# Three one-pass products in place of one float32 product for layer 3's maps, and grouped float32r products in layer 4

## The chip, the cores and the metric

The kernel runs on one core of a Trainium2 chip. The metric is the time of one execution on the device in microseconds (us), as the median of several runs. TensorE (PE) multiplies matrices, VectorE (DVE) and ScalarE (ACT) work element by element, GpSimd (POOL) does a little of that, and SyncE (SP) issues nearly all DMAs from one queue, in the order in which they are written. Each engine runs its own instructions in order; semaphores tie the engines together.

## The reference

A graph with 3125 nodes of 256 features and 50000 edges goes through a layer norm, a relu and four SAGE layers; the input is added at the end.

```python
def _sage_conv(x, src, dst, Wl, Wr, b):
    agg = segment_sum(x[src], dst, num_segments=n)
    deg = segment_sum(ones_like(dst), dst, num_segments=n)
    mean = agg / maximum(deg, 1.0)[:, None]
    return mean @ Wl + x @ Wr + b
h = maximum(_layernorm(x), 0.0)
h = relu(_sage_conv(h, src, dst, Wl1, Wr1, b1))     # 256 -> 256
h = relu(_sage_conv(h, src, dst, Wl2, Wr2, b2))     # 256 -> 128
h = relu(_sage_conv(h, src, dst, Wl3, Wr3, b3))     # 128 -> 256
out = x + _sage_conv(h, src, dst, Wl4, Wr4, b4)     # 256 -> 256
```

## The kernel before

**Tiles and chunks.** The nodes are cut into 25 tiles of 128 (the last has 53) and into seven chunks: six of 512 nodes and one of 53. `ORDER` is 5, 6, 4, 3, 2, 1, 0; the text speaks of places, so place 1 is the short chunk (53 nodes) and places 0 and 2 to 6 are full. A dense table of edge counts, `counts`, stays on chip. Layer 1 is computed while this table is built; layers 2, 3 and 4 come after it, and this study is about layers 3 and 4.

**One place of a layer.** PE sums over all 25 source tiles (`add_sources`, called k = 0 to 24 by the loop `place` of the tensor block): for each tile the stored node values, as an f16 high part and an f16 low part, are multiplied by the counts, so a place of layer 3 is 49 products of 128x512 (the last tile takes one), and one of layer 4 is 98. The sums of a place lie in `agg_ps` or `window_ps`, in turn. DVE scales them by the reciprocal degrees into `aggT` (`scale_agg`, L1570). Then come the layer's two dense maps of the sums (`aggT`) and of the chunk's own values (`selfT`), called `lin`. PE issues `lin` of place q between the tiles of place q+1; the tables `rest` and `first_rests` say behind which tile k. In layer 3 that is k = 6 for place 2 and later, and place 2 carries two, `lin(3, 0)` at k = 2 and `lin(3, 1)` at k = 15, since place 1 is too short to hold any. The `lin` and the turns of the last place stand in the first place of the next layer, ahead of the tiles that `REST_AT` names.

**Layer 3 before.** `lin(3, q)` is four float32 products for a full chunk: two halves h of the 256 outputs, each W3 times `aggT` and W3 times `selfT`, in `lin_ps` (L2297). ACT makes the relu from `lin_ps` to `newT` (L1923) and an f16 high part (`high_part`, L1940); DVE makes the f16 low part (`low_part`, L1591). SP stores `newT` to memory (`hT_d`) and turns the four parts from feature-major to node-major by DMA transposes (`move_turned`, L913); places 1 and 6 are turned by PE instead (`turn`) and copied by DVE (`copy_turned`, L1608). On SP the order for place q is: wait for `lin`, load `selfT` of place q+1 (L852), load the reciprocal degrees of place q+1 (L864), store `newT`, issue the four transposes. So a load of `selfT` stands behind the transposes of the place before. DVE's order in layer 3 is `scale_agg(q)`, then for each half `low_part` and `copy_turned`; ACT's is the two relus, then the two high parts.

**Layer 4 before.** Its maps are already made with one-pass products. An operand a and a weight w are split into f16 parts and a sum part; eight f16 products of 256 columns give one half of the bank `last_ps(i)` and four float32r products of 256 columns (L2268) the other, tile by tile; DVE joins the two with fixed factors (`add_out`, L1692 and L1697). `split_operand` (L1733, L1737) and ACT's `operand_parts` (L2039) make the parts.

Of the kernel before, what the change touches and what calls it, by code (L numbers as in the profile page):

```python
# [26 lines left out]
def sage_stack_kernel(nc, x, src, dst, Wl1, Wr1, b1, Wl2, Wr2, b2, Wl3, Wr3, b3, Wl4, Wr4, b4, out):  # L27
# [240 lines left out]
    with ctx:  # L268
# [75 lines left out]
        partsT = sb("partsT", [P, 2, CH], f16)  # L344
        newH = sb("newH", [P, TPC, 2, D], f16)
        rdeg = sb("rdeg", [P, CH], f32)
        ident16 = sb("ident16", [P, P], f16)
        columns = sb("columns", [P, 18], f32)
# [4 lines left out]
        unscale_high, unscale_sum, unscale_up = (columns[:, i:i + 1] for i in (15, 16, 17))  # L353

# [252 lines left out]
        W4_parts = sem("W4_parts")  # L607
        W4_rests = sem("W4_rests")
# [13 lines left out]
        LIN = [0, 2, 1, 2, TPC]  # L622
# [56 lines left out]

        def in_second(l, q, h):  # L680

            return l == 3 and h == 1 and by_dma(q)
# [34 lines left out]
        REST_AT = {1: (2, 6, 11), 2: (2, 10), 3: (2, 6, 9)}  # L717
# [450 lines left out]
        def _(dve):  # L1168
# [417 lines left out]
            def low_part(l, q, h):  # L1586
                n, t = size_of(chunk_at(q))
                dve.wait_ge(high_done[l], TURNS[l] * q + h + 1)
                parts = parts_of(l, q, h)
                low = parts[:, 1, 0:n] if n == CH else parts[:, 0, TWIN:TWIN + n]  # L1590
                v.scalar_tensor_tensor(out=low, in0=(lin_ps if l == 1 else newT)[:, h, 0:n],  # L1591
                                       scalar=1 / SPLIT if l == 3 else scale[:, l - 1:l], in1=parts[:, 0, 0:n], op0=ALU.mult,
                                       op1=ALU.subtract).then_inc(low_done[l], 1)
# [107 lines left out]
            def scale_columns():  # L1701

                order.after(v.tensor_single_scalar(scale_up, scale[:, 2:3], SPLIT, ALU.mult))
                v.tensor_scalar(bias3_up, bT[:, 3:5], scale_up, None, ALU.mult)
                v.tensor_single_scalar(unscale_high, unscale[:, 3:4], (1 - 1 / SPLIT) / W4_UP, ALU.mult)
                v.tensor_single_scalar(unscale_sum, unscale[:, 3:4], 1 / SPLIT / W4_UP, ALU.mult)
                order.after(v.tensor_single_scalar(unscale_up, unscale[:, 3:4], 1 / SPLIT, ALU.mult))

            def split_weights():

                dve.wait_ge(W4_parts, 2)
# [5 lines left out]
                dve.wait_ge(lin_done[3], 2 * NCH)  # L1717
# [5 lines left out]
                for of in range(2):  # L1723
                    v.tensor_tensor(W4_rest[:, of, :, :], W4_sums[of][:, :, :].bitcast(f32), W4_high[of], ALU.subtract
                                    ).then_inc(W4_rests, 1)

            def split_operand(of, q):
# [3 lines left out]
                for k in range(2):  # L1731
                    dve.wait_ge(operand_high, 4 * q + 2 * (1 - of) + k + 1)
# [64 lines left out]
        def _(act):  # L1797
# [104 lines left out]
            def relu(l, q):  # L1902
                n, t = size_of(chunk_at(q))
                bias = {1: 0, 2: 2, 3: 3}[l]
# [7 lines left out]
                for h in range(NEW[l]):  # L1912
# [9 lines left out]
                    if l == 3:  # L1922
                        a.activation(newT[:, h, 0:n], source, ACT.Relu, bias=bias3_up[:, h:h + 1], scale=scale_up  # L1923
                                     ).then_inc(relu_done[l], 1)
                        continue
                    a.activation(newT[:, h, 0:n], source, ACT.Relu, bias=bT[:, bias + h:bias + h + 1]  # L1926
                                 ).then_inc(relu_done[l], 1)

            def high_part(l, q, h):
# [7 lines left out]
                else:  # L1937
# [3 lines left out]
                             scale=1 / SPLIT if l == 3 else scale[:, l - 1:l]).then_inc(high_done[l], 1)  # L1941
# [79 lines left out]

            for l in (2, 3):
                def place(q, bank):
                    relu(l, q)
# [32 lines left out]
        def _(pe):  # L2057
# [193 lines left out]
            def last_maps(q):  # L2251
# [3 lines left out]
                if isinstance(q, int) and q == 0:  # L2255
                    pe.wait_ge(W4_parts, 6)
                pe.wait_ge(operand_low, 4 * (q + 1))
                if not isinstance(q, int) or q > 0:
                    pe.wait_ge(out_made, both(q, TPC, 1))
                for i in range(t):  # L2260
                    node, wide = slice(i * P, i * P + rows_), slice(i * P, (i + 1) * P)
# [3 lines left out]
                    for j, (h, w) in enumerate(products):  # L2265
                        m(last_ps(i)[0:rows_, 0:D], h, w, start=(j == 0), stop=(j == len(products) - 1))  # L2266
                    for j, (of, k) in enumerate(((1, 0), (1, 1), (0, 0), (0, 1))):
                        last = m(last_ps(i)[:, D:2 * D], last_sums[:, of, k, wide], W4_sums[of][:, k, :],  # L2268
                                 start=(j == 0), stop=(j == 3))
                    last.then_inc(lin_done[4], 1)  # L2270

            def lin(l, q):

                if l == 4:
                    last_maps(q)
                    return
                n, t = size_of(chunk_at(q))
# [4 lines left out]
                if l == 3 and isinstance(q, int) and q == 0:  # L2282
                    pe.wait_ge(late_loaded, LATE)
# [6 lines left out]
                for h in range(1 if l == 2 else 2):  # L2290
                    cols = slice(h * P, (h + 1) * P)
                    if l == 2:
                        ops = [(Wr2_sb[:, k, :], selfT[:, k, 0:n]) for k in range(2)]
                    else:
                        ops = [(W3[:, 0, cols], aggT[:, 0, 0:n]), (W3[:, 1, cols], selfT[:, 0, 0:n])]
                    for i, (w, r) in enumerate(ops):
                        last = m(lin_ps[:, h, 0:n], w, r, start=(i == 0), stop=(i == len(ops) - 1))  # L2297
                    last.then_inc(lin_done[l], 1)
# [198 lines left out]
            def rest(l, q):  # L2497
# [3 lines left out]
                        3: {6: [lambda: lin(3, q)], 16: [lambda: turn(3, q, 0)], 22: [lambda: turn(3, q, 1)]},  # L2501
                        4: {8: [lambda: lin(4, q)]}}[l]

            def first_rests(l):
# [3 lines left out]
                        3: {2: [lambda: lin(3, 0)], 8: [lambda: turn(3, 0, 0)], 12: [lambda: turn(3, 0, 1)],  # L2508
                            15: [lambda: lin(3, 1)]},
                        4: {2: [lambda: lin(4, 0)], 12: [lambda: lin(4, 1)]}}[l]  # L2510

            for l in (2, 3, 4):
                def place(q, bank):
# [3 lines left out]
                    if l == 3 and isinstance(q, int) and q == 3:  # L2517
                        between = {2: [lambda: turn(3, 1, 0)], 5: [lambda: turn(3, 1, 1)], **between}
# [83 lines left out]
```

## Time and profile before

| | |
|---|---|
| median of 3 runs | 645.88 us (645.56 to 646.54) |
| the profiled execution | 645.63 us, of which the span from the first to the last instruction is 643.8 us |
| PE busy | 615.5 us, 96% of the span |
| DVE busy, ACT busy | 318.9 us (50%), 194.1 us (30%) |
| granted clock of PE, mean | 0.986 |

The profile is one execution. In it layer 3 begins at 383.9 us of the span; place 1 begins at 397.10, place 2 at 398.34. Matmuls are pipelined: the duration of one contains some 0.16 us that the next one overlaps, so the pace of PE is read from the distance of two starts, not from the duration. A line of the timeline merges consecutive instructions of one kind (xN), with the time from the first start to the last end. A float32 product of 128x512 shows as two records.

### The profile page before, as it was taken

Reading aid. Unit: us, or ns where it says so; the run is one execution under the profiler, and the core shown is the slowest. Engines: PE = TensorE matmul, PEld = TensorE weight load, DVE = VectorE, ACT = ScalarE, POOL = GpSimd, SP = SyncE. Lnnn points to the kernel's source line nnn. Section 1 sums busy time; section 2 is a strip of 40 time slices with the busy share of each in tenths; the row PEclk is TensorE's granted clock in tenths of the full one; section 3 lists DMA queues with packets and bytes.
Section 4 is the critical chain, followed back from the end, with each engine's and each line's share of the span. In section 5 each row is a group of like instructions: output and inputs, shape, how many; then the busy total and the mean of one; then the engine's idle time right before and its main releaser. Section 6 shows DMA issues by size and latency. Waiting matters only on the chain.

```text
span 643.8 us, 10273 instructions
## 1 busy us (share of the span) xinstructions
PE 615.5 (96%) x4155; PEld 339.3 (53%) x4156; DVE 318.9 (50%) x616; ACT 194.1 (30%) x411; POOL 41.8 (6%) x91
## 2 busy tenths in 40 slices
PE   5678999999999999999999999999999999999998
PEld 4435555656555555554444445444445646556586
DVE  6977876878888779721211111111126343334421
ACT  3876866365653622300111001122122010000100
POOL 8001300000000000000000000000002020110110
PEclk9977999999999999999999999999999999999999
DMA  8401200510210202142433531534451133030330
GB/s 265 104 1 46 85 1 3 184 57 6 68 53 15 88 23 83 34 139 67 147 89 89 151 86 50 106 98 111 140 126 33 43 86 113 2 115 10 105 116 33
DMA packets 59687, 51.00 MB, mean 79 GB/s; under 512 B 31670, under 2 KB 44507, under 8 KB 59640
## 3 DMA queue, kind: packets, MB, share of 16 engines
q1 hardware_dynamic: 59284, 49.74, 26.8%
q8 instruction: 33, 0.54, 0.3%
q0 software_dynamic: 240, 0.37, 0.2%
q10 hardware_dynamic: 116, 0.24, 0.1%
q14 instruction: 14, 0.11, 0.1%
HBM read 28.15 MB, written 16.60 MB: 70 GB/s over the span
## 4 chain that ended last, share of the span: by engine, by line
PE 86%; DVE 6%; ACT 3%; DMA 2%; issue 2%; POOL 1%; SPq 0%; DVEq 0%; ACTq 0%; POOLq 0%
PE agg_ps L2362 34%; PE window_ps L2362 19%; PE lin_ps L2297 5%; PE window_ps L2183 5%; PE lin_ps L2246 3%; PE lin_ps L2140 2%; PE agg_ps L2338 2%; PE lin_ps L2266 2%; PE lin_ps L2305 2%; DVE early L1479 1%; PE lin_ps L2384 1%; PE degree_ps L2061 1%; PE turn_ps L2183 1%; PE window_ps L2338 1%; ACT counts L1876 1%
## 5 line engine op out<-in xcount | busy, mean ns | idle before, releaser
L2362 PE MATMUL agg_ps<-counts,H 128*128 128x512 f16 (+2 forms) x1026 | 235.1, 355 | 1.0 <-DVE aggT L1570 0.8
L2362 PEld LDWEIGHTS agg_ps<-counts,H 128*128 128x128 f16 (+1 forms) x1026 | 79.2, 98 | 56.2 <-issue 10.2
L1876 ACT ACTIVATE counts<-window_ps 128x400 f16<-128x400 f32 x150 | 73.5, 506 | 62.8 <-PE window_ps L2183 49.7
L1472 DVE TENSOR_TENSOR counts<-early 128x2048 f16<-128x2048 bf16 x66 | 78.0, 1213 | 7.2 <-PE window_ps L2183 4.8
L2362 PE MATMUL window_ps<-counts,early 128*128 128x512 f16 (+2 forms) x346 | 77.8, 379 | 0.0
L2362 PEld LDWEIGHTS window_ps<-counts,early 128*128 128x128 f16 (+1 forms) x346 | 33.5, 98 | 41.3 <-issue 3.4
L2362 PE MATMUL window_ps<-counts,H 128*128 128x512 f16 (+1 forms) x291 | 55.2, 346 | 0.0
L2183 PEld LDWEIGHTS window_ps<-counts 128*128 128x128 f16 x412 | 30.9, 99 | 33.2 <-issue 4.6
L1472 DVE TENSOR_TENSOR early<-early 128x1024 f16<-128x1024 bf16 (+1 forms) x69 | 43.9, 684 | 7.6 <-PE window_ps L2183 6.1
L2362 PE MATMUL agg_ps<-counts,early 128*128 (+4 forms) x297 | 46.5, 314 | 0.0
L2183 PE MATMUL window_ps<-counts 128*128 128x100 f16 x412 | 41.4, 210 | 1.0 <-DVE counts L1472 0.8
L1926 ACT ACTIVATE newT<-newT,columns 128x512 f32<-128x512 f32 (+1 forms) x21 | 13.4, 663 | 90.6 <-DVE newT L1754 66.2
L1134 POOL TENSOR_TENSOR newH<-newH,plan 128x256 f32<-128x256 f32 (+1 forms) x25 | 18.3, 760 | 334.2 <-DMA newH<-in_x_dram 334.2
L2183 PE MATMUL window_ps<-early 128*128 128x100 f16 (+1 forms) x256 | 33.1, 229 | 7.0 <-DVE early L1479 5.3
L2362 PEld LDWEIGHTS window_ps<-counts,H 128*128 128x128 f16 x291 | 24.7, 97 | 28.6 <-issue 1.1
L2183 PEld LDWEIGHTS window_ps<-early 128*128 128x128 f16 x256 | 21.7, 102 | 33.7 <-ACT counts L1876 6.9
L1570 DVE SCALAR_TENSOR_TENSOR aggT<-agg_ps,columns,rdeg 128x512 f32<-128x512 f32 (+1 forms) x21 | 13.7, 679 | 46.5 <-PE agg_ps L2362 43.4
L2362 PEld LDWEIGHTS agg_ps<-counts,early 128*128 128x128 f16 (+1 forms) x297 | 22.0, 97 | 24.3 <-issue 1.1
L1923 ACT ACTIVATE newT<-lin_ps,columns 128x512 f32<-128x512 f32 (+1 forms) x14 | 10.1, 723 | 66.8 <-PE lin_ps L2297 62.5
L2039 ACT ACTIVATE H<-selfT 128x512 f16<-128x512 f32 (+1 forms) x12 | 6.1, 557 | 70.5 <-DMA selfT<-hT_d 70.5
L1591 DVE SCALAR_TENSOR_TENSOR partsT<-newT,partsT 128x512 f16<-128x512 f32 (+1 forms) x9 | 5.3, 587 | 44.1 <-ACT partsT L1940 43.9
L2246 PE MATMUL lin_ps<-aggT,W 128*128 128x512 f32 (+1 forms) x56 | 25.1, 564 | 0.6 <-DVE aggT L1570 0.6
(302 smaller groups left out, 712.5 us busy)
## 6 DMA issues: line engine op xcount, KB each, us to landing
selfT<-hT_d SPq DMA_DIRECT2D x18, 512.0 KB, 4.2
hT_d<-newT SPq DMA_DIRECT2D x12, 512.0 KB, 4.6
rdeg<-rdeg_d SPq DMA_DIRECT2D x22, 256.0 KB, 4.1
counts<-in_x_dram SPq DMA_DIRECT2D x6, 512.0 KB, 8.1
hT_d<-counts SPq DMA_DIRECT2D x6, 512.0 KB, 3.6
newH<-in_x_dram SPq DMA_DIRECT2D x6, 512.0 KB
out_dram<-newT SPq DMA_DIRECT2D x5, 512.0 KB
hT_d<-newT SPq DMA_DIRECT2D x6, 256.0 KB, 3.8
```

The costliest lines, as they stand in the source:

```text
L1134: nc.gpsimd.tensor_tensor(x4[0:q, i, :], x4[0:q, i, :], b4rows[0:q, :], ALU.add).then_inc(x4_biased, 1)
L1472: v.tensor_tensor(hots_of(group).rearrange("p r a (n d) -> p r a n d", d=2), pairs.unsqueeze(1).unsqueeze(1).broadcast_to([P, n, 2, P // 2 ...
L1570: v.scalar_tensor_tensor(out=aggT[:, h, 0:n], in0=(agg_ps, window_ps)[bank][:, h, 0:n], scalar=SPLIT if l == 4 else unscale[:, l - 1:l], i ...
L1876: a.activation(counts[:, :, 2 * w * WIN:2 * (w + 1) * WIN].rearrange("p t (a w) -> p a t w", a=2), window_bank(FILL_AT[w])[:, 0:2 * KEYS]. ...
L1926: a.activation(newT[:, h, 0:n], source, ACT.Relu, bias=bT[:, bias + h:bias + h + 1]).then_inc(relu_done[l], 1)
L2140: last = m(h0_ps(j)[h][:, 0:n], W14[:, 1, k, h * P:(h + 1) * P], x_T[c][:, k, 0:n], start=(k == 0), stop=(k == 1))
L2183: m(window_bank(at)[:, key0:key0 + keys], one_src, one_key, start=(j == 0), stop=(j == STEPS[w] - 1)).then_inc(hot_used, 1)
L2246: last = m(lin_ps[:, h, 0:n], W14[:, 0, k, h * P:(h + 1) * P], aggT[:, k, 0:n], start=(k == 0), stop=(k == 1))
L2266: m(last_ps(i)[0:rows_, 0:D], h, w, start=(j == 0), stop=(j == len(products) - 1))
L2297: last = m(lin_ps[:, h, 0:n], w, r, start=(i == 0), stop=(i == len(ops) - 1))
L2338: last = m((agg_ps, window_ps)[bank][:, h, cols], tile[:, part, h * P:(h + 1) * P], counts[0:rows_, k, c * CH + g * HALF_CH:c * CH + (g + ...
L2362: last = m((agg_ps, window_ps)[bank][:, h, 0:n], tile[:, part, h * P:(h + 1) * P], counts[0:rows_, k, chunk_cols(c, n)], start=first and p ...
```

## The change

Layer 3's maps are made as layer 4's are. W3, `aggT` and `selfT` are each split into an f16 high part, an f16 low part and a float32r sum. `lin(3, q)` becomes `third_maps`: for each half h four f16 products in `lin_ps`, and then for each half two float32r products in two other banks. DVE joins them in `newT` (`join_third`: `lin_ps` times 2047, plus the float32r sums), and ACT's relu reads `newT` in place of `lin_ps`. DVE splits the operands (`split_third`), ACT makes their high parts (`third_part`). The split of W3 stands in layer 2. The scales move: layer 2's relu multiplies by the scale of its f16 parts, so that what layer 3 loads is already scaled, and the high and low parts of layer 2 take a constant factor.

The places of `lin(3, q)` among the tiles move from k = 2, 15, 6 to k = 4, 19, 9; the one of place 2 stands at k = 18 of place 3, with the turns of place 1 at 4 and 7. `REST_AT[3]` moves from (2, 6, 9) to (4, 9, 12). In layer 4 all tiles' f16 products of a chunk come first and then all their float32r products.

```diff
-        REST_AT = {1: (2, 6, 11), 2: (2, 10), 3: (2, 6, 9)}
+        REST_AT = {1: (2, 6, 11), 2: (2, 10), 3: (4, 9, 12)}
...
-                                           scalar=SPLIT if l == 4 else unscale[:, l - 1:l], in1=rdeg[:, 0:n], op0=ALU.mult,
+                                           scalar=SPLIT if l > 2 else unscale[:, l - 1:l], in1=rdeg[:, 0:n], op0=ALU.mult,
...
+            def split_third_weights():
+
+                dve.wait_ge(weight_parts, 1)
+                order.after(v.scalar_tensor_tensor(out=W3_rest, in0=W3, scalar=W4_UP, in1=W3_high, op0=ALU.mult,
+                                                   op1=ALU.subtract))
+                order.after(v.scalar_tensor_tensor(out=W3_sums[:, :, :], in0=W3_rest, scalar=SPLIT, in1=W3_high,
+                                                   op0=ALU.mult, op1=ALU.add))
+                v.tensor_tensor(W3_rest, W3_sums[:, :, :].bitcast(f32), W3_high, ALU.subtract).then_inc(weight_rests, 1)
+
+            def split_third(of, q):
+
+                n, t = size_of(chunk_at(q))
+                dve.wait_ge(operand_high, 2 * q + 2 - of)
+                order.after(v.scalar_tensor_tensor(out=third_sums[:, of, 0:even(n)], in0=third_high[of][:, 0:even(n)],
+                                                   scalar=1 - SPLIT, in1=(aggT, selfT)[of][:, 0, 0:even(n)],
+                                                   op0=ALU.mult, op1=ALU.add))
+                v.tensor_tensor(third_low[of][:, 0:n], third_sums[:, of, 0:n].bitcast(f32), third_high[of][:, 0:n],
+                                ALU.subtract).then_inc(operand_low, 1)
+
+            def join_third(q):
+
+                n, t = size_of(chunk_at(q))
+                dve.wait_ge(hT_stored[3], 16 * q) if q > 0 else dve.wait_ge(hT_stored[2], 16 * NCH)
+                for h in range(2):
+                    dve.wait_ge(lin_done[3], LIN[3] * q + h + 1)
+                    ins = v.tensor_single_scalar(newT[:, h, 0:n], lin_ps[:, h, 0:n], SPLIT - 1, ALU.mult)
+                order.after(ins)
+                for h in range(2):
+                    dve.wait_ge(lin_done[3], LIN[3] * q + 2 + h + 1)
+                    v.tensor_tensor(newT[:, h, 0:n], third_sums_ps[h][:, 0:n], newT[:, h, 0:n], ALU.add
+                                    ).then_inc(summed, 1)
...
+                    if l == 2 and q == 2:
+                        split_third_weights()
+                    if l == 3:
+                        split_third(1, q)
                     if l == 4:
                         split_operand(1, q)
                     scale_agg(l, q, bank)
+                    if l == 3:
+                        split_third(0, q)
+                        join_third(q)
...
-                        act.wait_ge(lin_done[l], NEW[l] * q + h + 1)
-                        source = lin_ps[:, h, 0:n]
+                        act.wait_ge(summed, NCH + NEW[l] * q + h + 1)
+                        source = newT[:, h, 0:n]
...
+            def third_part(of, q):
+
+                n, t = size_of(chunk_at(q))
+                act.wait_ge(self_loaded[3], 16 * (q + 1)) if of else act.wait_ge(agg_scaled[3], q + 1)
+                a.activation(third_high[of][:, 0:even(n)], (aggT, selfT)[of][:, 0, 0:even(n)], ACT.Copy, scale=1 / SPLIT
+                             ).then_inc(operand_high, 1)
...
+                    if l == 2 and q == 1:
+                        act.wait_ge(late_loaded, LATE)
+                        a.activation(W3_high, W3, ACT.Copy, scale=W4_UP).then_inc(weight_parts, 1)
+                    if l == 2 and q == 4:
+                        act.wait_ge(weight_rests, 1)
+                        a.activation(W3_low, W3_rest, ACT.Copy, scale=-1 / SPLIT).then_inc(weight_parts, 1)
+                    if l == 3:
+                        third_part(1, q)
+                        third_part(0, q)
                     relu(l, q)
...
                         m(last_ps(i)[0:rows_, 0:D], h, w, start=(j == 0), stop=(j == len(products) - 1))
+                for i in range(t):
+                    wide = slice(i * P, (i + 1) * P)
                     for j, (of, k) in enumerate(((1, 0), (1, 1), (0, 0), (0, 1))):
                         last = m(last_ps(i)[:, D:2 * D], last_sums[:, of, k, wide], W4_sums[of][:, k, :],
...
+            def third_maps(q):
+
+                n, t = size_of(chunk_at(q))
+                if q == 0:
+                    pe.wait_ge(weight_parts, 2)
+                pe.wait_ge(operand_low, 2 * (q + 1))
+                if q > 0:
+                    pe.wait_ge(relu_done[3], NEW[3] * q)
+                halves = [slice(h * P, (h + 1) * P) for h in range(2)]
+                for h, cols in enumerate(halves):
+                    products = [(w[:, of, cols], part[of][:, 0:n]) for of in (1, 0)
+                                for w, part in ((W3_high, third_high), (W3_low, third_low))]
+                    for j, (w, r) in enumerate(products):
+                        last = m(lin_ps[:, h, 0:n], w, r, start=(j == 0), stop=(j == len(products) - 1))
+                    last.then_inc(lin_done[3], 1)
+                for h, cols in enumerate(halves):
+                    for of in (1, 0):
+                        last = m(third_sums_ps[h][:, 0:even(n)], W3_sums[:, of, cols], third_sums[:, of, 0:even(n)],
+                                 start=(of == 1), stop=(of == 0))
+                    last.then_inc(lin_done[3], 1)
...
-                        3: {6: [lambda: lin(3, q)], 16: [lambda: turn(3, q, 0)], 22: [lambda: turn(3, q, 1)]},
+                        3: {9: [lambda: lin(3, q)], 18: [lambda: turn(3, q, 0)], 22: [lambda: turn(3, q, 1)]},
...
-                        3: {2: [lambda: lin(3, 0)], 8: [lambda: turn(3, 0, 0)], 12: [lambda: turn(3, 0, 1)],
-                            15: [lambda: lin(3, 1)]},
+                        3: {4: [lambda: lin(3, 0)],
+                            19: [lambda: lin(3, 1)]},
...
-                        between = {2: [lambda: turn(3, 1, 0)], 5: [lambda: turn(3, 1, 1)], **between}
+                        between = {4: [lambda: turn(3, 1, 0)], 7: [lambda: turn(3, 1, 1)], 18: between[9]}
```

## Rows read from the trace of the kernel before

**Rows 1.** Page, parts 1 and 2: busy us and share; granted clock in 40 slices.

```profile
PE 615.5 (96%) x4155; PEld 339.3 (53%) x4156; DVE 318.9 (50%) x616; ACT 194.1 (30%) x411; POOL 41.8 (6%) x91
...
PEclk9977999999999999999999999999999999999999
```

**Rows 2.** Page, part 4: the chain that ended last, share of the span by engine.

```profile
PE 86%; DVE 6%; ACT 3%; DMA 2%; issue 2%; POOL 1%; SPq 0%; DVEq 0%; ACTq 0%; POOLq 0%
```

**Rows 3.** Windows view, places 1 to 6 of layer 3: length, busy us, clock.

```profile
397.10:470.20 73.10, 72.56 (x346) 33.84 (x345) 11.30 (x20) 14.21 (x24) 0.00 (x0) 1.00 0.45 108
```

**Rows 4.** Timeline, layer 3: start, us, engine, line, [idle before <-releaser].

```profile
397.10 1.40 PE L2362 MATMUL window_ps<-counts,H 128*128 128x53 f16 x49
397.38 0.75 DVE L1570 SCALAR_TENSOR_TENSOR aggT<-agg_ps,columns,rdeg 128x512 f32<-128x512 f32 x1 [5.85 <-PE agg_ps L2362]
...
398.34 1.46 PE L2362 MATMUL agg_ps<-counts,H 128*128 128x512 f16 x6
...
399.63 1.02 PE L2297 MATMUL lin_ps<-aggT,plan 128*128 128x512 f32 x2
...
403.07 5.78 PE L2362 MATMUL agg_ps<-counts,H 128*128 128x512 f16 x26
...
404.59 0.69 DVE L1591 SCALAR_TENSOR_TENSOR partsT<-newT,partsT 128x512 f16<-128x512 f32 x1 [6.47 <-ACT partsT L1940]
...
409.51 3.83 PE L2362 MATMUL agg_ps<-counts,H 128*128 128x512 f16 x17
...
412.53 0.25 ACT L1940 ACTIVATE partsT<-newT 128x53 f16<-128x53 f32 x1 [2.43 <-DMA early<-H]
...
417.02 1.12 PE L2297 MATMUL lin_ps<-aggT,plan 128*128 128x512 f32 x2 [0.54 <-DVE aggT L1570]
...
420.56 7.72 PE L2362 MATMUL window_ps<-counts,H 128*128 128x512 f16 x35
```

**Rows 5.** Timeline, layer 4: PE in the first maps of a chunk.

```profile
500.70 0.27 PE L2266 MATMUL lin_ps<-early,H 128*128 128x256 f16 x1
...
501.46 0.27 PE L2266 MATMUL lin_ps<-Wl_sb,aggT 128*128 128x256 f16 x1
...
502.04 0.28 PE L2266 MATMUL lin_ps<-early,H 128*128 128x256 f16 x1
...
506.14 7.08 PE L2362 MATMUL window_ps<-counts,H 128*128 128x512 f16 x32
```

**Rows 6.** Groups by shape, 395 us to the end: xcount, busy us, mean ns.

```profile
L1923 ACT ACTIVATE newT<-lin_ps,columns 128x512 f32<-128x512 f32 x12 | 9.3, 777 | 62.5 <-PE lin_ps L2297 62.5
...
L1733 DVE SCALAR_TENSOR_TENSOR last_sums<-H,aggT 128x512 fp32r<-128x512 f16 x10 | 6.6, 698 | 0.5
...
L1737 DVE TENSOR_TENSOR aggT<-last_sums,H 128x512 f16<-128x512 f32 x10 | 6.5, 688 | 0.2
L2039 ACT ACTIVATE H<-aggT 128x512 f16<-128x512 f32 x10 | 6.1, 631 | 34.9 <-DVE aggT L1570 34.9
...
L1570 DVE SCALAR_TENSOR_TENSOR aggT<-window_ps,rdeg 128x512 f32<-128x512 f32 x6 | 3.9, 686 | 9.8 <-PE window_ps L2362 9.8
...
L2268 PEld LDWEIGHTS lin_ps<-W_sums_agg,last_sums 128*128 128x128 f32 x22 | 3.4, 188 | 0.0
```

**Rows 7.** Groups by shape, DVE in layer 2.

```profile
L1754 DVE TENSOR_TENSOR newT<-lin_ps,aggT 128x512 f32<-128x512 f32 x6 | 4.1, 692 | 20.5 <-PE lin_ps L2297 20.5
```

**Rows 8.** Groups, 474 to 492 us, where POOL and DVE work together.

```profile
L1134 POOL TENSOR_TENSOR newH<-newH,plan 128x256 f32<-128x256 f32 x4 | 3.7, 948 | 210.9 <-DMA newH<-in_x_dram 210.9
...
L1724 DVE TENSOR_TENSOR H<-W_sums_own,early 128x512 f32<-128x512 f32 x1 | 1.2, 1222 | 0.0
```

**Rows 9.** Timeline, SP's queue in layer 3: start, us of issuing.

```profile
405.31 3.40 SPq L913 DMA_TRANSPOSE early<-partsT  x2
...
411.38 0.58 SPq L852 DMA_DIRECT2D selfT<-hT_d  x1
```

**Rows 10.** DMA view: one kind of issue, KB, median us to landing.

```profile
selfT<-hT_d SPq DMA_DIRECT2D x6, 256.0 KB, 2.7
```

More of the change, by code:

```diff
@@ L344, in sage_stack_kernel @@
         partsT = sb("partsT", [P, 2, CH], f16)
+        with nc.sbuf_tensor("third_sums", [P, 2, CH], f32r) as third_sums:
+            pass
         newH = sb("newH", [P, TPC, 2, D], f16)
@@ L347, in sage_stack_kernel @@
         ident16 = sb("ident16", [P, P], f16)
-        columns = sb("columns", [P, 18], f32)
+        columns = sb("columns", [P, 21], f32)
         bT = columns[:, 0:5]
@@ L353, in sage_stack_kernel @@
         unscale_high, unscale_sum, unscale_up = (columns[:, i:i + 1] for i in (15, 16, 17))
+        scale_up2, bias2_up, rescale3 = (columns[:, i:i + 1] for i in (18, 19, 20))
         upper = newH[:, TPC // 2:TPC, :, :].rearrange("p t h f -> p (t h f)")
@@ L621, in sage_stack_kernel @@
         TURNS = [0, 1, 1, 2, 0]
[L622 removed]
+        LIN = [0, 2, 1, 4, TPC]
         NW = 12
@@ L678, in sage_stack_kernel, with even @@
         W4_rest = raw[:, 0:2 * 4 * D].bitcast(f32).rearrange("p (o k n) -> p o k n", o=2, k=2)
+        third_high, third_low = ([tile[:, 1, :].bitcast(f16)[:, a:a + CH] for tile in (aggT, selfT)] for a in (0, CH))
+        W3_high = early[:, BEHIND:BEHIND + 2 * D].rearrange("p (a n) -> p a n", a=2)
+        W3_low = spare_low.rearrange("p (a n) -> p a n", a=2)
+        W3_sums = W4_sums_own
+        W3_rest = raw[:, HALF:HALF + 4 * D].bitcast(f32).rearrange("p (a n) -> p a n", a=2)
+        third_sums_ps = (degree_ps, agg_ps[:, 1, :])
+        def even(n):
+            return n + n % 2
         def in_second(l, q, h):
@@ L1591, in low_part @@
                 v.scalar_tensor_tensor(out=low, in0=(lin_ps if l == 1 else newT)[:, h, 0:n],
-                                       scalar=1 / SPLIT if l == 3 else scale[:, l - 1:l], in1=parts[:, 0, 0:n], op0=ALU.mult,
+                                       scalar=1 / SPLIT if l > 1 else scale[:, l - 1:l], in1=parts[:, 0, 0:n], op0=ALU.mult,
                                        op1=ALU.subtract).then_inc(low_done[l], 1)
@@ L1701, in scale_columns @@
             def scale_columns():
+                v.tensor_single_scalar(scale_up2, scale[:, 1:2], SPLIT, ALU.mult)
                 order.after(v.tensor_single_scalar(scale_up, scale[:, 2:3], SPLIT, ALU.mult))
+                v.tensor_scalar(bias2_up, bT[:, 2:3], scale_up2, None, ALU.mult)
+                v.scalar_tensor_tensor(out=rescale3, in0=scale_up, scalar=1 / SPLIT / W4_UP, in1=unscale[:, 2:3],
+                                       op0=ALU.mult, op1=ALU.mult)
                 v.tensor_scalar(bias3_up, bT[:, 3:5], scale_up, None, ALU.mult)
@@ L1919, in relu @@
                     else:
-                        act.wait_ge(lin_done[l], NEW[l] * q + h + 1)
-                        source = lin_ps[:, h, 0:n]
-                    if l == 3:
-                        a.activation(newT[:, h, 0:n], source, ACT.Relu, bias=bias3_up[:, h:h + 1], scale=scale_up
-                                     ).then_inc(relu_done[l], 1)
+                        act.wait_ge(summed, NCH + NEW[l] * q + h + 1)
+                        source = newT[:, h, 0:n]
+                    if l > 1:
+                        a.activation(newT[:, h, 0:n] if l == 3 else newT[:, 0, 0:n], source, ACT.Relu,
+                                     bias=bias3_up[:, h:h + 1] if l == 3 else bias2_up,
+                                     scale=rescale3 if l == 3 else scale_up2).then_inc(relu_done[l], 1)
                         continue
-                    a.activation(newT[:, h, 0:n], source, ACT.Relu, bias=bT[:, bias + h:bias + h + 1]
-                                 ).then_inc(relu_done[l], 1)
+                    a.activation(newT[:, h, 0:n], source, ACT.Relu, bias=bT[:, h:h + 1]).then_inc(relu_done[l], 1)
             def high_part(l, q, h):
@@ L2275, in lin @@
                     last_maps(q)
+                    return
+                if l == 3:
+                    third_maps(q)
                     return
@@ L2289, in lin @@
                     return
[L2290 to L2298, printed above, removed]
+                for k in range(2):
+                    last = m(lin_ps[:, 0, 0:n], Wr2_sb[:, k, :], selfT[:, k, 0:n], start=(k == 0), stop=(k == 1))
+                last.then_inc(lin_done[l], 1)
             def narrow_part(q, k):
```

32 lines of the change are left out of this document (14 added, 18 removed).

## The prediction

> **What bounds the kernel now.** First the page: TensorE is busy for 96% of the span, at a granted clock of 9 tenths or more in all slices but two early ones [rows 1], and the chain that ended last runs through PE for 86% [rows 2]. Then the windows by stage: in places 1 to 6 of layer 3 PE is busy for 72.6 of 73.1 us at clock 1.00 (2.4 GHz), DVE for 11.3, ACT for 14.2, POOL for nothing [rows 3]. So here the time is the sum of PE's products plus any wait of PE. The timeline then gives the pace by distances of starts: 6 products of 512 f16 columns in 1.29 us, 0.216 each; 49 of 53 columns in 1.24, 0.025 each [rows 4]. It also shows PE's one real wait in layer 3: after 31 products and two turns from 409.51 the maps of place 2 could start near 416.3, and start at 417.02 behind DVE's scaling [rows 4]. DVE was held by place 1, whose high part waited for transposes. What the change does to PE's products is easily priced; what decides is whether the longer road through ACT and DVE still fits between two of PE's starts.
>
> **The products.** The four float32 products of a full chunk take 403.07 - 399.63 = 3.44 us [rows 4]. In their place stand eight f16 products of 512 columns, 8 x 0.216 = 1.73, and four float32r ones. Layer 4 shows those at 256 columns: f16 runs at 0.76 / 7 = 0.109, and from the last f16 product to the next tile are 0.58, so four float32r take 0.47, 0.118 each [rows 5]. That is close to one column a clock, so 512 columns cost 0.216 at least and 2 x 0.118 = 0.237 at most; I take 0.216, since what is over in the 0.118 looks like a fixed cost. Sum 2.59 (2.68): a gain of 0.85 (0.76) for each of six chunks, 5.1 us (4.6). Place 1: from 403.07 + 26 x 0.216 = 408.69 to 409.51 are 0.82 now [rows 4]; 8 x 0.025 + 4 x 0.118 = 0.67 then, a gain of 0.15.
>
> **Layer 4's grouping.** A tile takes (506.14 - 500.70) / 4 = 1.36, while 8 x 0.109 + 4 x 0.118 is 1.344 [rows 5]: changing kinds costs at most 0.02 a tile. Three of four changes go in five chunks: 0.2 us gained, between 0 and 0.3. The first tile's result comes later for `add_out`, but the last one's does not, and the next chunk's maps are a place away: nothing.
>
> **Work on DVE and ACT.** Eight more DVE steps (four of `split_third`, four of `join_third`) and two more of ACT per chunk. DVE's prices: 0.70 and 0.69 for the split, 0.69 for the scaling [rows 6], 0.69 for an addition that reads PSUM [rows 7]; independent steps follow each other every 0.61 to 0.65 (10 in 6.5), dependent ones after some 0.04 (0.2 idle in five pairs), and ACT to DVE costs 0.1 at most [rows 6]. ACT: 0.63 for a high part, 0.78 for a relu with two columns [rows 6]. DVE comes to about 45 of 70 us, so as a whole it bounds nothing. The product of `join_third`, one f32 source in PSUM, has no row: between half of 0.69 and all of it, and I take all, the nearest row being [rows 7]. The Trainium skill, VectorE: DVE Perf Modes, "Why PSUM operands drop a tier", has any f32 operand from PSUM at the base rate, which agrees; at half the price the wait below would be 0.3 shorter.
>
> The split of W3 (three DVE steps, two of ACT) stands in layer 2, where DVE has ten free microseconds a place; if it were late, `scale_agg` of that place is queued behind it, 1.3 us once. The three tiny column steps are far from any wait.
>
> **Chain 1, end of a place to its maps.** 0.28 until DVE starts [rows 4], scaling 0.69, ACT 0.63, split 0.70 + 0.69, hand-overs 0.15: 3.15. PE gets there in 20 products, 4.3, so no wait. At place 0 it is place 1's 1.24 plus 10 x 0.216 = 3.4, and in layer 4's first place 16 x 0.216 = 3.45: just enough, 0.25 spare.
>
> **Chain 2, maps to maps, from a start S of `third_maps`.** Half 0's f16 products end at S + 0.86, half 1's at 1.73, the sums at 2.16 and 2.59; each is readable 0.28 later. DVE's second product runs 2.0 to 2.7, the additions to 3.4 and 4.05; relus 3.45 to 4.9; high parts to 5.4 and 5.9; low parts to 6.15 and 6.75 (before: a low part started 404.59 - 399.63 = 4.96 after the maps [rows 4]; now at 5.45). The next `split_third(1)` stands behind those on DVE: to 8.1. The scaling to 8.7, ACT to 9.35, `split_third(0)` to 10.8, PE at S + 10.9. The `selfT` load (2.7 us [rows 10], issued near S + 2.9) is in time. Between two maps at k = 9 PE needs 2.59 + 49 x 0.216 = 13.2: no wait. But from k = 18 of place 3 to k = 9 of place 4 it is 2.59 + 31 x 0.216 = 9.3. There PE waits 10.9 - 9.3 = **1.6 us**, with what is open above between 0.9 and 2.3. It is not given back, as all behind it is PE work.
>
> **Chain 3, to the maps of place 2.** From S of place 0: first transposes at S + 6.15; SP reaches the load of `selfT` 6.07 later [rows 9]; landing 2.7 to 3; then ACT 0.63, split 1.35, scaling 0.69, ACT 0.63, split 1.4, hand-overs 0.2: S + 20.0. PE arrives after 2.59 + 77 x 0.216 + 0.67 + two turns, S + 20.0. A tie; so is turn 1 (high part 7.2 after the first transpose [rows 4, 9], then 0.5: S + 13.85, PE S + 13.9). Today's wait of 0.7 there (between 0.54, the row's idle, and 0.8) goes; I put 0.2 in its place, between 0 and 1.5, the time of one more transpose (6.07 / 4).
>
> **Sum.** -5.1 - 0.15 - 0.2 - 0.7 + 1.6 + 0.2 = -4.35. The profiled execution took 645.63, 0.25 under the median of the runs shown: 641.3 for it, **641.5 us** by the median. With the products' other end and the waits' it is 640.7 to 642.4.
>
> **Rivals.**
>
> *Late hand-overs at places 1 and 2.* Chain 3 hangs on SP's queue and four transposes, and both its meetings are ties; one transpose late adds 1.5 at once, with nothing to absorb it. For it: a high part already waits 2.43 for a transpose [rows 4]. Against: the loads ahead of the transposes go out earlier than before. 643.0, up to 644.2.
>
> *No wait at place 3.* If chain 2 were 1.6 shorter, 639.9. For it: independent steps of DVE and ACT overlap by a tenth or so. Against: it is eleven steps in series.
>
> *The float32r products take two passes at 512 columns.* Then 0.43 each, the maps cost 3.45 as now, and PE meets place 3 later, so that wait is 1.1: -1.05 + 1.1 + 0.2, or 646.1. Against it the 0.118 of [rows 5].
>
> *The float32r weight loads stand in the open.* A load takes 0.188 [rows 6]; 24 of them unhidden are 4.5, less 0.6 of the wait: 645.4. The pace of 0.118 under a load of 0.188 [rows 5, 6] says that they overlap. The Trainium skill, TensorE: Matmul & The Clock Gate, "What overlaps and what doesn't", lets a load overlap a running product only in another row group; by that rule this case would hold, and the trace does not agree.
>
> *DVE steps at double price (the slower side).* Beside POOL one DVE step took 1.22 [rows 8]. If layer 3's steps ran so, chain 2 gains some 4.5 and is 15.4, over PE's 13.2 at every place: 1.6 + 4.5 + 2.2 + 2.2 + 3.1 of waits, about 653. From a mean step of 0.95 on the waits eat the gain. Against: POOL is idle in layer 3 [rows 3].
>
> **Chances.** The forecast 0.60; late hand-overs 0.22; no wait 0.08; two passes 0.04; open loads 0.02; dear DVE steps 0.04. A measurement of this kernel tells about 0.2% (1.3 us) from no change. Faster by more: 0.60 + 0.20 + 0.08 = 0.88; within: 0.02 + 0.03 + 0.02 = 0.07; slower: 0.04 + 0.01 = 0.05. The range 640.1 to 643.8 leaves out half of "no wait", the far end of the late hand-overs and the last three cases, 0.17.
>
> **What would show it.** Maps of 2.6 us per chunk with starts 0.216 apart, float32r too; PE idle near 1.6 us ahead of `third_maps` of place 3, released by DVE's second `split_third`, and little ahead of place 2 and the first turn; no idle at places 4 to 6; layer 4's chunk maps about 0.06 shorter. Wrong would be: starts of float32r products 0.4 apart, idle of PE at every place, DVE steps well over 0.7, or a wait ahead of place 0 or 6, where only 0.25 is spare.

## The result, and the profile after

| | before | after |
|---|---|---|
| median of 6 runs each | 645.72 us (644.87 to 647.79) | 641.36 us (640.37 to 642.83) |
| ratio, with its 95% interval | | 0.9932 (0.9911 to 0.9952) |
| the profiled execution, its span | 645.63, 643.8 | 640.37, 638.4 |
| from place 1 of layer 3 to the end of the span | 246.7 | 242.4 |

The forecast was 641.5 us. The last row of the table is the better ruler. The two spans differ by 5.4 us, but 1.07 of that lies ahead of place 1 of layer 3 (it begins at 396.03 instead of 397.10), in stages that the change hardly touches; 0.92 of it stands already ahead of layer 1's last maps (303.74 instead of 304.66). In the other profiles of this study place 1 begins anywhere from 396.23 to 398.76. From place 1 to the end the gain is 246.7 - 242.4 = 4.3 us, and this length is called the stretch below. Of all timed runs one is left out of the figures: the tenth of experiment 7, which took 1260.52 us at a recorded clock of 1.00, where the other nine took 643 to 646.

The page of the kernel after, parts 1 and 2: busy us with its share, and the granted clock in 40 slices. They answer to [rows 1].

```profile
PE 609.6 (95%) x4183; PEld 339.0 (53%) x4184; DVE 353.3 (55%) x678; ACT 202.4 (32%) x427; POOL 44.5 (7%) x91
...
PEclk9977999999999999999999999999999999999999
```

The windows by stage of the kernel after: length, then busy us (and instructions) of PE, PEld, DVE, ACT and POOL, then PE's clock, DMA share and GB/s. The line is places 1 to 6 of layer 3 and answers to [rows 3].

```profile
396.03:466.56 70.53, 69.14 (x373) 33.54 (x372) 39.32 (x69) 20.17 (x36) 0.00 (x0) 1.00 0.39 110
```

DVE's work here went from 11.3 to 39.3 us and ACT's from 14.2 to 20.2, and the stage got 2.6 us shorter (73.10 to 70.53): both still fit beside PE. But PE, which had 0.5 us of idle time, now has 1.4. The waits view of PE, from layer 3 to the end, says where: who waited for whom, us in total, times, the longest.

```profile
PE lin_ps L2360 <- DVE aggT L1763: 1.4, 1, 1.4
PE degree_ps L2438 <- DVE aggT L1833: 0.4, 1, 0.4
```

One wait in layer 3, once, behind DVE's second step of `split_third`. (The second line stands at the end of layer 4, outside the change.) The timeline of the kernel after shows the maps of place 0, those of place 1, the end of chain 3 at the maps of place 2, and DVE's chain up to that wait; it answers to [rows 4].

```profile
396.03 1.39 PE L2453 MATMUL window_ps<-counts,H 128*128 128x53 f16 x49
...
399.42 0.38 PE L2360 MATMUL lin_ps<-selfT,early 128*128 128x512 f16 x1
...
400.93 0.38 PE L2360 MATMUL lin_ps<-aggT,Wl_sb 128*128 128x512 f16 x1
...
400.96 0.83 PE L2364 MATMUL degree_ps<-third_sums,W_sums_own 128*128 128x512 f32 x2
...
401.63 0.62 PE L2364 MATMUL agg_ps<-third_sums,W_sums_own 128*128 128x512 f32 x2
...
402.09 6.65 PE L2453 MATMUL agg_ps<-counts,H 128*128 128x512 f16 x30
...
408.58 0.19 PE L2360 MATMUL lin_ps<-selfT,early 128*128 128x53 f16 x1
...
409.24 2.12 PE L2453 MATMUL agg_ps<-counts,H 128*128 128x512 f16 x9
...
418.54 0.69 DVE L1763 TENSOR_TENSOR aggT<-third_sums,aggT 128x512 f16<-128x512 f32 x1
...
419.51 0.38 PE L2360 MATMUL lin_ps<-selfT,early 128*128 128x512 f16 x1
...
425.04 0.69 DVE L1607 SCALAR_TENSOR_TENSOR partsT<-newT,partsT 128x512 f16<-128x512 f32 x1 [1.59 <-ACT partsT L1998]
425.65 0.69 DVE L1607 SCALAR_TENSOR_TENSOR H<-newT,H 128x512 f16<-128x512 f32 x1
...
426.25 0.68 DVE L1760 SCALAR_TENSOR_TENSOR third_sums<-selfT 128x512 fp32r<-128x512 f16 x1
426.97 0.69 DVE L1763 TENSOR_TENSOR selfT<-third_sums,selfT 128x512 f16<-128x512 f32 x1
427.58 0.68 DVE L1586 SCALAR_TENSOR_TENSOR aggT<-window_ps,rdeg 128x512 f32<-128x512 f32 x1
428.30 0.63 ACT L2084 ACTIVATE aggT<-aggT 128x512 f16<-128x512 f32 x1 [2.25 <-DVE aggT L1586]
...
428.96 0.69 DVE L1760 SCALAR_TENSOR_TENSOR third_sums<-aggT 128x512 fp32r<-128x512 f16 x1 [0.70 <-ACT aggT L2084]
429.69 0.69 DVE L1763 TENSOR_TENSOR aggT<-third_sums,aggT 128x512 f16<-128x512 f32 x1
...
430.43 0.39 PE L2360 MATMUL lin_ps<-selfT,early 128*128 128x512 f16 x1 [1.39 <-DVE aggT L1763]
```

Read it so. The maps of a full chunk last from 399.42 to 402.09, 2.67 us. Their eight f16 products start 0.216 apart (400.93 - 399.42 = 7 x 0.216). From the last f16 start, 400.93, to the next tile, 402.09, are 1.16; less 0.216 for that f16 product, the four float32r products take 0.944, 0.236 each, with the changes of kind in it. (A float32r record can start while the product before it still runs, so the first of them, at 400.96, doesn't mark the pace.) Place 1's maps take 409.24 - 408.58 = 0.66. At the maps of place 2, DVE is done at 419.23 and PE starts at 419.51 without idle. DVE's first low part starts at 425.04, behind ACT's high part. From there DVE works without a pause through the low parts, the split of `selfT` and the scaling, hands `aggT` to ACT and gets it back 0.70 later, and PE starts the maps of place 3 at 430.43, 10.92 after those of place 2.

Layer 4's first maps of a chunk, in PE's timeline of the kernel after, beside [rows 5]: 32 f16 products from 495.69, 16 float32r ones, the next tile at 501.06.

```profile
495.69 0.27 PE L2339 MATMUL lin_ps<-early,H 128*128 128x256 f16 x1
...
499.07 0.27 PE L2339 MATMUL turn_ps<-Wl_sb,aggT 128*128 128x256 f16 x1
499.10 0.48 PE L2343 MATMUL lin_ps<-W_sums_own,last_sums 128*128 128x256 f32 x2
499.42 0.40 PE L2343 MATMUL lin_ps<-W_sums_agg,last_sums 128*128 128x256 f32 x2
...
500.82 0.39 PE L2343 MATMUL turn_ps<-W_sums_agg,last_sums 128*128 128x256 f32 x2
501.06 1.25 PE L2453 MATMUL window_ps<-counts,H 128*128 128x512 f16 x5
```

That is 5.37 us where it was 5.44, and the time from place 1 of layer 4 to the end of the span went from 148.20 to 147.80.

Last, the groups by shape for 396 to 467 us of the kernel after (xcount, busy us, mean ns, idle before), with the two steps that [rows 6] did not have and the float32r weight loads.

```profile
L1981 ACT ACTIVATE newT<-newT,columns 128x512 f32<-128x512 f32 x10 | 7.6, 806 | 27.6 <-DVE newT L1776 27.6
L1772 DVE TENSOR_SCALAR newT<-lin_ps 128x512 f32<-128x512 f32 x10 | 6.9, 691 | 9.3 <-PE lin_ps L2360 8.8
...
L2364 PEld LDWEIGHTS degree_ps<-third_sums,W_sums_own 128*128 128x128 f32 x12 | 2.2, 190 | 0.7
```

### The profile page after: what moved, and what is told of

Same layout as the page of the kernel before. It is cut to its first block, busy times and chain, and to the rows that moved or that the text cites. A ratio compares the mean times of both kernels' runs of the same rounds, so it can differ in the third digit from the quotient of the medians.

```text
span 638.4 us, 10420 instructions
## 1 busy us (share of the span) xinstructions
PE 609.6 (95%) x4183; PEld 339.0 (53%) x4184; DVE 353.3 (55%) x678; ACT 202.4 (32%) x427; POOL 44.5 (7%) x91
## 4 chain that ended last, share of the span: by engine, by line
PE 86%; DVE 7%; ACT 3%; issue 2%; DMA 1%; POOL 1%; SPq 0%; DVEq 0%; ACTq 0%; POOLq 0%
PE agg_ps L2453 34%; PE window_ps L2453 19%; PE window_ps L2256 5%; PE lin_ps L2319 4%; PE lin_ps L2213 2%; PE lin_ps L2388 2%; PE lin_ps L2360 2%; PE agg_ps L2429 2%; PE lin_ps L2396 2%; PE lin_ps L2339 2%; PE turn_ps L2256 1%; DVE early L1495 1%; PE lin_ps L2475 1%; PE degree_ps L2134 1%; PE window_ps L2429 1%
## 5 line engine op out<-in xcount | busy, mean ns | idle before, releaser
L1981 ACT ACTIVATE newT<-newT,columns 128x512 f32<-128x512 f32 (+1 forms) x21 | 15.2, 754 | 100.7 <-DVE newT L1813 65.2
L1586 DVE SCALAR_TENSOR_TENSOR aggT<-agg_ps,columns,rdeg 128x512 f32<-128x512 f32 (+1 forms) x17 | 10.7, 663 | 30.9 <-PE agg_ps L2453 27.8
L1708 DVE SCALAR_TENSOR_TENSOR newT<-lin_ps,columns,newH 128x256 f32<-128x256 f32 (+1 forms) x11 | 4.9, 479 | 37.8 <-PE lin_ps L2343 37.8
L1495 DVE TENSOR_TENSOR early<-early 128x384 f16<-128x384 bf16 (+2 forms) x64 | 21.7, 397 | 6.6 <-PE window_ps L2256 5.9
```

The costliest lines, as they stand in the source:

```text
L1495: last = v.tensor_tensor(hot.rearrange("p (r n d) -> p r n d", r=n, d=2), numbers_to[:, 0:size].rearrange("p (n d) -> p n d", d=2).unsquee ...
L1981: a.activation(newT[:, h, 0:n] if l == 3 else newT[:, 0, 0:n], source, ACT.Relu, bias=bias3_up[:, h:h + 1] if l == 3 else bias2_up, scale= ...
```

## Experiments

The theory after the result: the time from place 1 on is the sum of PE's products plus waits of PE ahead of `third_maps`. Each wait ends when the chain through PE, DVE and ACT ends: chain 2 (maps to maps, 10.9) or chain 3 (place 0's maps to place 2's). Rivals: a chunk is slowed by DVE's load as a whole; the positions behind the tiles matter little; the grouping in layer 4 gives nothing. Experiments 1 to 4 ran beside 17 runs of the kernel before (median 646.24), 5 to 7 later on the same chip beside 12 (646.70). Diffs are against the changed kernel.

**1. Place 3's maps four tiles later.** The change moved `third_maps` of place 2 to k = 18 and left place 3's at k = 9, 31 tile products behind. Moved to k = 13, PE has eight products more to do first.

```diff
+                    if l == 3 and isinstance(q, int) and q == 4:
+                        between = {13: between[9]}
```

> The changed kernel with the maps of place 3 at k = 13 of place 4 in place of k = 9. Theory (PE waits there because the road from the maps of place 2 through DVE and ACT takes 10.9 us, and nothing else is late): eight more products, 1.73 us, stand before them, so the wait of 1.56 goes and no other comes, since from k = 13 to k = 9 of the next place are still 2.67 + 41 x 0.216 = 11.5 us. From place 1 of layer 3 to the end of the span 242.4 - 1.6 = 240.8 us. Rival (the wait is of something that comes at a fixed time after place 3's end, or DVE as a whole is the bound): PE waits again ahead of these maps or of those of place 4, and the stretch stays at 242.4.

Measured: 639.43 us (639.13 to 641.17), ratio 0.9888 (0.9873 to 0.9902); stretch 240.81. PE's timeline of this kernel: the tiles between the maps of place 2 and those of place 3, and the first product of the latter.

```profile
426.95 6.21 PE L2453 MATMUL agg_ps<-counts,H 128*128 128x512 f16 x28
432.99 0.38 PE L2360 MATMUL lin_ps<-selfT,early 128*128 128x512 f16 x1
```

No idle time stands before 432.99, 11.09 after the maps of place 2 (at 421.90), against a chain of 10.92. The 1.56 us of the wait are gained whole, no later place waits for the four tiles, and this is the best version of the study: it beats both kernels.

**2. Layer 4 tile by tile again.** One line taken out, so that a tile's float32r products follow its f16 ones as before.

```diff
-                for i in range(t):
                     wide = slice(i * P, (i + 1) * P)
```

> The changed kernel with layer 4's float32r products back behind each tile's f16 products. Theory (a change of kind costs some 0.02 us): the maps of a full chunk go from 5.37 back to 5.44 us, 0.35 to 0.4 us over five chunks, too little for the times to tell and seen in the trace alone: 242.8 us from place 1 of layer 3 to the end. Rival (grouping matters for add_out or for the next chunk): over 1 us.

Measured: 641.21 us (640.68 to 644.00), ratio 0.9923 (0.9906 to 0.9940); stretch 242.78. From place 1 of layer 4 to the end it is back at 148.19. So the grouping is worth 0.39 us, seen in the trace; the median cannot show so little.

**3. The old positions.** The products of the change, but `lin` behind the tiles of the kernel before (k = 2, 15, 6; turns at 2, 5, 16, 22; `REST_AT` 2, 6, 9), without the move to k = 18.

```diff
-        REST_AT = {1: (2, 6, 11), 2: (2, 10), 3: (4, 9, 12)}
+        REST_AT = {1: (2, 6, 11), 2: (2, 10), 3: (2, 6, 9)}
...
-                        3: {9: [lambda: lin(3, q)], 18: [lambda: turn(3, q, 0)], 22: [lambda: turn(3, q, 1)]},
+                        3: {6: [lambda: lin(3, q)], 16: [lambda: turn(3, q, 0)], 22: [lambda: turn(3, q, 1)]},
...
-                        3: {4: [lambda: lin(3, 0)],
-                            19: [lambda: lin(3, 1)]},
+                        3: {2: [lambda: lin(3, 0)],
+                            15: [lambda: lin(3, 1)]},
...
-                        between = {4: [lambda: turn(3, 1, 0)], 7: [lambda: turn(3, 1, 1)], 18: between[9]}
+                        between = {2: [lambda: turn(3, 1, 0)], 5: [lambda: turn(3, 1, 1)], 6: between[6]}
```

> The changed kernel with layer 3's maps and turns at the old places (k = 2 and 15 of place 2, 6 behind, and 2, 6, 9 in layer 4's first place). Theory (the products gain 0.77 us a chunk only where the longer road fits ahead of them): PE waits 0.6 us at place 0, 4.1 at place 2, 0.1 at each of places 3 to 5, 1.4 at place 6, and the 1.56 of place 3 goes: 4.9 us slower than the changed kernel, 247.3 us from place 1 to the end, about 646 in all, the time before the change. Rival (the gain is the products' alone and the places matter little): 641 to 642.5.

Measured: 648.51 us (648.23 to 650.10), ratio 1.0041 (1.0027 to 1.0054); stretch 249.83. The positions decide the sign. PE's waits in this kernel:

```profile
PE lin_ps L2360 <- DVE aggT L1763: 5.9, 3, 4.1
PE turn_ps L2415 <- DVE partsT L1607: 0.4, 1, 0.4
```

In the timeline the idle times are 0.53 at place 0, 4.07 at place 2, 1.27 at place 6 and 0.41 at a turn: meetings that the prediction had as ties or near them, but for place 2, whose maps here come 12 tiles earlier. Each delays PE by its idle time and 0.16 of pipelining, 6.9 in all, so these waits alone would give 242.4 - 1.56 + 6.9 = 247.7. The stretch is 2.1 longer than that. Some of it is in three waits too short to show as idle time, ahead of the maps of places 3, 4 and 5, which the expectation had. The first of them in the timeline of this kernel:

```profile
423.96 7.73 PE L2453 MATMUL window_ps<-counts,H 128*128 128x512 f16 x35
431.53 3.19 PE L2453 MATMUL agg_ps<-counts,H 128*128 128x512 f16 x14
...
433.94 0.69 DVE L1763 TENSOR_TENSOR aggT<-third_sums,aggT 128x512 f16<-128x512 f32 x1
434.69 0.39 PE L2360 MATMUL lin_ps<-selfT,early 128*128 128x512 f16 x1
```

The 49 products from 423.96 end at 434.54, DVE at 434.63, and the maps start at 434.69, 0.15 late. The maps at 448.10 and 461.50 are as late, 0.45 in all. The windows view of this kernel around the longest wait (the columns as above):

```profile
415.60:419.66 4.06, 0.00 (x0) 0.00 (x1) 3.24 (x5) 0.63 (x1) 0.00 (x0) 1.00 0.00 0
419.66:421.00 1.34, 1.34 (x5) 0.56 (x6) 0.10 (x1) 0.00 (x0) 0.00 (x0) 0.81 0.00 0
421.00:423.00 2.00, 2.00 (x6) 1.26 (x5) 1.06 (x2) 0.00 (x0) 0.00 (x0) 0.50 0.00 0
423.00:425.00 2.00, 2.00 (x8) 0.89 (x8) 1.61 (x3) 0.74 (x2) 0.00 (x0) 0.78 0.00 0
```

After the wait PE's granted clock falls to 0.50, the lower of its two levels (1.2 of 2.4 GHz). The time lost is 1.34 x 0.19 + 2.00 x 0.50 + 2.00 x 0.22 = 1.7 us. With the 0.45 that accounts for the 2.1. The expectation had the waits to within 1 us; the clock it didn't have.

**4. Place 2's maps at k = 9.** Only the move to k = 18 is undone.

```diff
-                        between = {4: [lambda: turn(3, 1, 0)], 7: [lambda: turn(3, 1, 1)], 18: between[9]}
+                        between = {4: [lambda: turn(3, 1, 0)], 7: [lambda: turn(3, 1, 1)], 9: between[9]}
```

> The changed kernel with the maps of place 2 at k = 9 of place 3, as at the other places, and not at k = 18. Theory: they meet the road over the transposes, the load of selfT and DVE 3.88 us earlier, with 0.2 spare, so PE waits 3.7 there; from there to place 3's maps it is a whole place, 13.2 us, so the 1.56 of place 3 goes: 2.1 us slower than the changed kernel, 244.5 us from place 1 to the end. Rival (the place of these maps only shifts one wait): the two waits add up to 1.6 again and the stretch stays at 242.4.

Measured: 645.50 us (644.53 to 647.26), ratio 0.9988 (0.9976 to 0.9999); stretch 246.11. Place 3's wait is gone, and a wait ahead of place 2 has taken its place; it delays PE by 3.66 (from 417.12, where the tile products end, to 420.78). That alone gives 242.4 - 1.56 + 3.66 = 244.5, as expected. The other 1.6 are the clock again, in the windows view of this kernel:

```profile
417.10:420.78 3.68, 0.19 (x1) 0.00 (x1) 2.86 (x5) 0.63 (x1) 0.00 (x0) 1.00 0.00 0
420.78:421.60 0.82, 0.82 (x4) 0.41 (x5) 0.00 (x0) 0.00 (x0) 0.00 (x0) 0.99 0.00 0
421.60:425.00 3.40, 3.40 (x10) 1.79 (x7) 1.79 (x3) 0.00 (x0) 0.00 (x0) 0.50 0.00 0
425.00:440.00 15.00, 15.00 (x70) 7.05 (x70) 8.34 (x13) 4.68 (x8) 0.00 (x0) 1.00 0.41 111
```

Of 3.40 us at half clock 1.7 are lost, and PE's timeline has its f16 products 0.427 apart in that stretch (421.72, 422.14, 422.57, 423.00) instead of 0.216.

**5 and 6. Two DVE steps more in one place.** `join_third`'s product of half 1 is made three times instead of once, with the same result, in series on DVE: in place 2 (experiment 5), ahead of the wait, or in place 3 (experiment 6), where PE has 13.2 us of work from one start of the maps to the next, more than chain 2 takes.

```diff
+                    for again in range(2 if q == 2 and h == 1 else 0):
+                        order.after(ins)
+                        ins = v.tensor_single_scalar(newT[:, h, 0:n], lin_ps[:, h, 0:n], SPLIT - 1, ALU.mult)
```

> The changed kernel with join_third's second product made three times, one after the other, in place 2 alone: 2 x 0.73 = 1.45 us more on the road from the maps of place 2 to those of place 3. Theory (that road is what PE waits for there): the wait grows from 1.56 to 3.0 us, 243.85 us from place 1 to the end; if a wait of 3.0 us costs PE its clock as the one of 3.7 us did, up to 1.7 more. Rival (PE waits there for something else, a load or the scaling): nothing changes, 242.4.

> The same two steps more, in place 3 alone. Theory (the road from maps to maps takes 10.9 us and PE comes after 13.25, so only a road that is over 2.3 us longer is felt): no wait ahead of place 4's maps, 242.4 us from place 1 to the end. Rival (DVE as a whole is what layer 3 waits for): 1.45 us more here as well, 243.85.

Measured: in place 2, 642.87 us (641.73 to 643.49), ratio 0.9941 (0.9920 to 0.9962), stretch 243.86, the wait ahead of place 3's maps longer by 1.45 and no other. In place 3, 641.00 us (639.87 to 642.64), ratio 0.9921 (0.9892 to 0.9950), stretch 242.38, nothing lost. So DVE's load as a whole bounds nothing. A step costs its whole price where chain 2 is the longer way, and none where PE is. The windows view of experiment 5 around its wait, which leaves PE without work for 2.85 us:

```profile
430.50:433.55 3.05, 0.20 (x1) 0.00 (x1) 2.26 (x4) 0.63 (x1) 0.00 (x0) 1.00 0.55 115
433.55:436.50 2.95, 2.95 (x14) 1.61 (x15) 1.67 (x3) 0.00 (x0) 0.00 (x0) 1.00 0.22 50
```

Here the clock does not fall.

**7. Place 2's maps at k = 12.** Six tile products more ahead of them than in experiment 4, so a wait of 2.4 instead of 3.7, shorter than the one of experiment 5. If the length of a wait decides on the clock, it stays up here.

```diff
+                        between = {4: [lambda: turn(3, 1, 0)], 7: [lambda: turn(3, 1, 1)], 12: between[9]}
```

> The changed kernel with the maps of place 2 at k = 12 of place 3, between the 18 of the change and the 9 that cost PE its clock. Theory (a wait costs its length, and the half clock came from the length of the wait): PE arrives 2.6 us earlier than at k = 18 and waits 2.4 us, the 1.56 of place 3 goes (11.9 us from there to place 3's maps), and if the clock stays at 1.00 the stretch from place 1 to the end is 240.8 + 2.4 = 243.2 us. Rival (any wait at this place costs the clock, whatever its length): 1.7 us more, 244.9.

Measured: 644.91 us (642.99 to 645.67, nine of ten runs), ratio 0.9972 (0.9957 to 0.9987); stretch 244.82. The windows view of this kernel:

```profile
417.10:419.48 2.38, 0.18 (x2) 0.01 (x1) 1.59 (x3) 0.63 (x1) 0.00 (x0) 1.00 0.00 0
419.48:420.40 0.92, 0.92 (x4) 0.40 (x5) 0.00 (x0) 0.00 (x0) 0.00 (x0) 0.90 0.00 0
420.40:423.40 3.00, 3.00 (x8) 1.79 (x7) 1.44 (x3) 0.00 (x0) 0.00 (x0) 0.50 0.00 0
```

The wait delays PE by 2.36 (417.12 to 419.48), as worked out (242.4 - 1.56 + 2.36 = 243.2), and the clock falls all the same: 0.92 x 0.10 + 3.00 x 0.50 = 1.6 more, 244.8. The theory that the length alone decides has fallen.

## Why the prediction was right

It was right in time (641.5 against 641.36) and in mechanism. Its terms, as the stretch shows them:

| term | forecast | measured | read from |
|---|---|---|---|
| products of six full chunks | -5.1 | -4.6 | 6 x (3.44 - 2.67) |
| place 1's maps | -0.15 | -0.16 | 0.82 - 0.66 |
| grouping in layer 4 | -0.2 | -0.4 | 148.20 - 147.80, and experiment 2 |
| the old wait at place 2 | -0.7 | -0.7 | no idle ahead of 419.51 |
| the new wait at place 3 | +1.6 | +1.56 | 10.92 against 9.36; experiment 1 |
| late hand-overs | +0.2 | 0 | no other wait of PE in layer 3 |
| sum | -4.35 | -4.3 | 246.7 to 242.4 |

**The products' term was mis-sized.** The step was the choice of 0.216 for a float32r product of 512 columns, "since what is over in the 0.118 looks like a fixed cost". It is not a fixed cost: at 512 columns one takes 0.236 (0.944 for four), at 256 columns 0.117 (twelve in 1.40, 499.42 to 500.82). The excess over f16 is 0.020 (0.014 if the 0.026 that a change of kinds costs, see below, is taken off the four) and 0.008, so from 256 to 512 columns it grows with the columns. The other end that the prediction kept, 0.237 and 0.76 a chunk, is what came. The error of 0.5 was covered by two small ones the other way, 0.2 in the grouping and 0.2 in the hand-overs. That the sum is better than its terms is luck. Experiment 1 tests the gains apart from the wait: 4.6 + 0.16 + 0.4 + 0.7 is 5.9, and its stretch, which has no wait in layer 3, is 246.7 - 240.8 = 5.9 shorter.

**The inner range.** The prediction's 640.7 to 642.4 is not the plain sum of its ends: with a wait of 0.9 it would be 640.8, with the products' other end and a wait of 2.3 it would be 642.7. The measured 641.36 lies in both.

**The grouping.** A change of kinds was bounded at 0.02 a tile, from the difference of 1.36 and 1.344, two rounded paces. The 0.4 over 15 changes that went (three in each of five chunks) make it 0.026, a little over the upper end.

**Chain 2** was forecast at 10.9 and measures 10.92. The steps came where they were put: the first low part at 425.04 (5.53 after the maps, forecast 5.45), the scaling's end at 428.26 (8.75, forecast 8.7). The product from PSUM, which had no row, takes 0.69 as the nearest row said. Experiments 5 and 6 show that it is this chain, at this one place, that costs. DVE's work in the six places came to 39.3 us where the prediction had about 45, which changes nothing: as a whole DVE bounds nothing, as it said.

**Chains 1 and 3** were ties or nearly so, and came out on the good side: 0.3 spare at place 0 (DVE done at 399.11, PE at 399.42), 0.3 at place 2, and 0.85 at the first turn (place 1's high part starts 6.35 after the first transpose, 412.00 - 405.65, and not 7.2). The late hand-overs had 0.22 of the chance; they did not come, neither here nor in the profiles of experiments 1, 2, 5 and 6, which have these meetings at the same tiles. At place 0 experiment 3 shows how little was to spare: with the maps two tiles earlier PE is idle for 0.53 there, and with all the old positions the change is slower than the kernel before by 0.4%. The split of W3 in layer 2 was hidden, as forecast: from layer 1's last maps to layer 2's last are 80.37 us before (304.66 to 385.03) and 80.27 after (303.74 to 384.01).

**The other rivals.** No wait at place 3: fell, the wait is there. Two passes for float32r: fell, 0.236 and not 0.43. Weight loads in the open: fell; a load takes 0.190 and the products of 256 columns still follow at 0.117, less than their own loads would take in series. The Trainium skill, TensorE: Matmul & The Clock Gate, "What overlaps and what doesn't", would have had these loads wait; the trace disagrees here too. DVE at double price: fell, 0.69 and not 1.2.

**What the prediction did not have** is the clock. It priced every wait at its length. For the change as it is that held, since its one wait left the clock at 1.00. For the neighbours it did not: a wait of 2.4 to 4.2 us ahead of place 2's maps costs 1.6 to 1.7 more.

## What to carry to other kernels

When one-pass products take the place of a slow one, the saving on PE is a multiplication; whether it is kept is decided by the longer road through the other engines, so work out for each pair of starts the chain's length and PE's work in between, and place the consumer behind enough tiles. A move that helps one pair shortens the next: here k = 18 for place 2 cured 3.7 us and opened 1.56 at place 3, which four tiles more closed for nothing. And a long wait of a busy PE can cost more than its length, so read the granted clock in the windows behind each wait.

## What the runs showed that was not expected

- A float32r product takes some 7% more time than an f16 one of the same shape: 0.117 us against 0.109 for 256 columns. For 512 it is 0.236 against 0.216, 9%, with the changes of kind in it. This was seen only where float32r products follow each other. With 54 columns a float32r product still takes 0.115 (place 1: 0.66 less 8 x 0.025 for the f16 products, over four). The prediction put the price of 256 columns there without a row of that shape, and it came out.
- In experiments 3, 4 and 7 waits that delayed PE by 4.2, 3.7 and 2.4 us ahead of place 2's maps put the granted clock to 0.50 for some 3.4 us, while 3.0 us ahead of place 3's (experiment 5) and 1.56 (the change) did not. Length alone does not decide. The fall came 24.0 to 24.1 us after the start of place 1 in all three. But as chain 3 ends these waits at the same moment (23.2 to 23.25), that is also 0.7 to 0.8 after PE's return in all three, so neither of the two is shown to be what counts. All timed runs of these three kernels had a mean clock of 0.984 (5, 12 and the 9 that count), and all four of experiment 5 had 0.987, so it is no accident of an execution. The Trainium skill, TensorE: Matmul & The Clock Gate, "What's actually happening", says that the window in which the chip watches PE's activity runs freely and doesn't begin with the kernel's work. By that a wait could cost in one execution and not in the next; these runs show no such spread, and what sets the fall stays open.
